# One selective-scan kernel: the outputs of two batch groups and the direct sums gathered in one PSUM bank

## What is computed

```python
dA  = jnp.exp(delta[..., None] * A)                  # 512 channels x 16 states
dBu = delta[..., None] * Bm[:, :, None, :] * xc[..., None]
def step(h, inp):
    da, dbu, c = inp
    h = da * h + dbu
    return (h, jnp.einsum('bdn,bn->bd', h, c))       # y of this step
_, ys = jax.lax.scan(step, h0, (dA, dBu, Cm))        # over 5 steps
y = ys + xc * D_skip
return y * jax.nn.silu(z) @ out_w.T
```

## Time and profile before

| what | us |
|---|---|
| median of 3 runs | 506.29 (503.71 to 507.09) |
| span of the profiled execution | 503.2 |
| scan, loop and its ends | about 291 to 438 of the span |
| after the scan | about 440 to 503.2 |

### The profile page before, as it was taken

How to read it: one execution, slowest core, us unless ns; L and a number is a source line. 1 busy time by engine, 2 the same in 40 slices (tenths; PEclk the granted TensorE clock), 3 DMA queues, 4 the chain that set the end, 5 groups by cost and what they waited for, 6 DMA issues and landing times.

```text
span 503.2 us, 6897 instructions
## 1 busy us (share of the span) xinstructions
PE 452.2 (90%) x1816; PEld 228.5 (45%) x1816; DVE 372.6 (74%) x709; ACT 236.0 (47%) x419; POOL 168.6 (34%) x164
## 2 busy tenths in 40 slices
PE   6999999999999999899967837988898888799997
PEld 3554655655554466477544501222222212275654
DVE  0257576566567668564999976899999999988756
ACT  1143323213221423355886945788887888421100
POOL 6000000100100021405450014889898989422000
PEclk9999999999999999997688977899999999999999
DMA  9992039100000000312026573366546655530000
GB/s 266 313 286 70 1 104 302 42 1 0 0 2 0 0 1 0 119 40 78 2 74 194 146 211 87 109 192 182 157 140 186 195 160 158 141 101 11 10 12 21
DMA packets 36344, 51.75 MB, mean 103 GB/s; under 512 B 5922, under 2 KB 26926, under 8 KB 36320
## 3 DMA queue, kind: packets, MB, share of 16 engines
q1 hardware_dynamic: 34736, 49.86, 33.9%
q10 hardware_dynamic: 1584, 1.59, 1.0%
HBM read 34.59 MB, written 16.52 MB: 102 GB/s over the span
## 4 chain that ended last, share of the span: by engine, by line
PE 33%; DVE 7%; SPq 6%; issue 5%; DMA 4%; ACT 3%; POOL 1%; DVEq 0%; POOLq 0%
PE ps L2072 7%; PE ps L1719 4%; PE ps L2039 4%; PE ps L1015 4%; DMA brows<-bparts 3%; PE ps L1672 3%; PE ps L1028 2%; PE ps L1685 2%; PE ps L1694 2%; SPq L1533 2%; PE ps L1060 2%; DVE da L1894 1%; PE ps L1703 1%; SPq L1007 1%; SPq L1610 1%
## 5 line engine op out<-in xcount | busy, mean ns | idle before, releaser
L1864 POOL TENSOR_TENSOR gb<-da,hb 128x512 f32<-128x512 f32 x62 | 77.8, 1277 | 61.7 <-ACT da L1784 55.2
L1784 ACT ACTIVATE da<-da 128x512 f32<-128x512 f32 x128 | 78.9, 629 | 24.8 <-DVE da L1894 20.4
L1894 DVE TENSOR_TENSOR da<-ps,expA 128x512 f32<-128x512 f32 x128 | 84.0, 686 | 7.8 <-PE ps L1672 7.1
L330 PE MATMUL ps<-area,convw 128*128 128x384 f32 (+1 forms) x220 | 73.4, 486 | 0.6 <-ACT peT L570 0.6
L397 PE MATMUL ps<-wall,peT 128*128 128x512 f32 x144 | 67.8, 593 | 0.0
L1672 PE MATMUL ps<-drows,selb 96*128 96x512 bf16 x128 | 48.5, 401 | 11.6 <-DVE da L1894 5.1
L330 PEld LDWEIGHTS ps<-area,convw 128*128 128x128 f32 (+1 forms) x220 | 41.2, 190 | 28.3 <-issue 1.4
L1685 PE MATMUL ps<-urows,brows 96*128 96x512 bf16 x96 | 35.0, 394 | 13.7 <-DVE gb L1901 7.6
L578 ACT ACTIVATE kvs<-ps 128x512 f32<-128x512 f32 x36 | 21.5, 597 | 52.6 <-PE ps L397 52.6
L570 ACT ACTIVATE peT<-ps 128x384 f32<-128x384 f32 x24 | 11.8, 491 | 66.4 <-PE ps L330 58.7
L1672 PEld LDWEIGHTS ps<-drows,selb 96*128 96x128 bf16 x128 | 11.4, 98 | 61.4 <-DVE da L1894 49.7
(11 more groups left out here) (242 smaller groups left out, 774.8 us busy)
## 6 DMA issues: line engine op xcount, KB each, us to landing
area<-in_xT SPq DMA_DIRECT2D x11, 768.0 KB
yscr<-yst SPq DMA_DIRECT2D x28, 208.0 KB
brows<-bparts SPq DMA_DIRECT2D x16, 240.0 KB, 3.0
drows<-dparts SPq DMA_DIRECT2D x14, 192.0 KB, 2.9
uparts<-pt SPq DMA_DIRECT2D x18, 128.0 KB, 2.4
dparts<-pt SPq DMA_DIRECT2D x18, 128.0 KB, 2.4
urows<-uparts SPq DMA_DIRECT2D x15, 144.0 KB, 2.9
inw<-in_in_wT SPq DMA_DIRECT2D x2, 1024.0 KB
```

The source lines that it names most:

```text
L330: mm = pe.matmul(bank(T_EMB + j % 2, 0, EN), convw[0:n, k, h * P:(h + 1) * P], xbuf[0:n, q, k, c * EN:(c + 1) * EN], start=(k == 0), stop= ...
L1784: act.activation(da_at(q, j), da_at(q, j), ACT.Exp, scale=-1.0).then_inc(da_ready, 1)
L1864: pool.tensor_tensor(gb_at(q, j), da_at(q, j), state, ALU.mult).then_inc({2: m2_done, 3: m3_done, 4: m4_done}[s_], 1)
L1894: dve.tensor_tensor(da_at(q, j), bank(j % 2), expA[:, j % 2, :], ALU.mult).then_inc(e_free, 1)
```

## The change

Outputs of both groups of a pair and the direct sums accumulate in the same bank. `cst` becomes 32 columns wide for each step: group q of a pair writes its C into columns 8q to 8q+8 of it, the rest is zero (set once by POOL before the scan). The four matmuls of q = 0 start the sums, those of q = 1 add to them, and `direct` adds its own into rows 16 to 31 of each block of 32 in bank 6. ACT copies the whole bank once per pair and k, at 128 rows, and `copy_direct` is gone. SP stores per pair: `store_y(i-1, 1)` in the first half, `store_y(i, 0)` and `store_k(i)` in the second; 14 transfers of 256 KB in place of 28 of 208 KB. In the last pair `send_y` carries the pair's 16 rows with one DMA for each j, and SP's order is `store_y(6, 1)`, the four DMAs of `gather_y(0)`, the four of `gather_y(1)`, then `send_y(0)`; after the loop follow the sends of k = 1. `yst` moves into the idle tile `inw`. The diff, cut to its core:

```diff
-        cst = sb("cst", [P, 2, 2, L + 1, GB], ctx=scn)
+        cst = sb("cst", [P, 2, 2, L + 1, 32], ctx=scn)
-            eng.wait_ge(landing(d, s_), 48 if s_ == 3 else 96)
+            eng.wait_ge(landing(d, s_), 32 if s_ == 3 else 64)
-        def send_y(eng, src, g, k, some=(0, 1, 2, 3)):
-            eng.wait_ge(y_copied[k], g + 1)
+        def send_y(eng, k, some=(0, 1, 2, 3)):
+            eng.wait_ge(y_copied[k], NPAIR)
...
-                eng.dma_start(ytok[g * GB:(g + 1) * GB, d, token(s_, d), :],
-                              src[32 * j:32 * j + GB, k, :]).then_inc(landing(d, s_), 16)
+                eng.dma_start(ytok[(NPAIR - 1) * PB:NPAIR * PB, d, token(s_, d), :],
+                              ylast[32 * j:32 * j + PB, k, :]).then_inc(landing(d, s_), 16)
...
-                    if last and q == 0:
-                        send_y(sp, yst, g, 0)
-                        store_y(g - 1, 1)
-                        gather_y(0, (0, 1, 2))
+                    if q == 0 and not first:
+                        store_y(i - 1, 1)
+                    if q == 0 and last:
+                        gather_y(0)
                     elif last:
-                        send_y(sp, ylast, g, 0)
-                        gather_y(0, (3,))
                         gather_y(1)
-                    else:
-                        store_y(g, 0)
-                        if not (first and q == 0):
-                            store_y(g - 1, 1)
-                    if q == 1 and not last:
+                        send_y(sp, 0)
+                    elif q == 1:
+                        store_y(i, 0)
                         store_k(i)
...
             def direct(i):
                 pe.wait_ge(da_ready, 16 * i + 16)
-                need(pe, y_copied[2], i)
...
-                        mm = pe.matmul(ps[o:o + GB, 5 * 512:6 * 512], cst[:, q, d, L, :], da_at(q, 6 + d),
-                                       start=True, stop=True)
+                        sums = cst[:, q, d, :, :].rearrange("p t m -> p (t m)")[:, 32 * L - PB:32 * L + PB]
+                        mm = pe.matmul(ps[o:o + 32, 6 * 512:7 * 512], sums, da_at(q, 6 + d),
+                                       start=False, stop=True, skip_group_check=True)
...
-            def outputs(g, q, k):
-                need(pe, y_copied[k], g)
+            def outputs(g, q, k, i):
+                if q == 0:
+                    need(pe, y_copied[k], i)
...
-                    mm = pe.matmul(ps[32 * j:32 * j + GB, (6 + k) * 512:(7 + k) * 512], cst[:, q, d, token(s_, d), :],
-                                   gb_at(q, 4 * k + j), start=True, stop=True)
+                    mm = pe.matmul(ps[32 * j:32 * j + 32, (6 + k) * 512:(7 + k) * 512], cst[:, q, d, token(s_, d), :],
+                                   gb_at(q, 4 * k + j), start=(q == 0), stop=(q == 1 and k == 1), skip_group_check=True)
...
-            def copy_y(g, k):
-                act.wait_ge(y_done[k], g + 1)
+            def copy_y(i, k):
+                act.wait_ge(y_done[k], 2 * i + 2)
+                if k == 0:
+                    act.wait_ge(y_done[2], i + 1)
...
-                    copy_y(g, 0)
                     if after:
                         exponential(g + 1, 1 - q, 2)
                     if q == 1:
-                        copy_direct(i)
+                        copy_y(i, 0)
                     if after:
                         exponential(g + 1, 1 - q, 3)
-                    if not (first and q == 0):
-                        copy_y(g - 1, 1)
+                    if q == 0 and not first:
+                        copy_y(i - 1, 1)
...
+            pool.wait_ge(xt_ready, NI)
+            pool.memset(cst[:, :, :, :, :], 0.0).then_inc(cleared, 1)
```

More of the change, by code:

```diff
@@ L1490, in tower @@
         y_done = [sem(f"y_done{k}") for k in range(3)]
-        y_copied = [sem(f"y_copied{k}") for k in range(3)]
+        y_copied = [sem(f"y_copied{k}") for k in range(2)]
         y_stored = [sem(f"y_stored{k}") for k in range(3)]
@@ L1516, in tower @@
         Y_ORDER = [(2, 3, 0, 1), (1, 0, 3, 2)]
[L1518 to L1519 removed]
+        PB = 2 * GB
+        def send_y(eng, k, some=(0, 1, 2, 3)):
+            eng.wait_ge(y_copied[k], NPAIR)
             for n in some:
@@ L1522, in send_y, with sums_row @@
                 d, s_ = j % 2, 2 * k + 1 + j // 2
-                eng.dma_start(ytok[g * GB:(g + 1) * GB, d, token(s_, d), :],
-                              src[32 * j:32 * j + GB, k, :]).then_inc(landing(d, s_), 16)
+                eng.dma_start(ytok[(NPAIR - 1) * PB:NPAIR * PB, d, token(s_, d), :],
+                              ylast[32 * j:32 * j + PB, k, :]).then_inc(landing(d, s_), 16)
+        def sums_row(q, d):
+            return 32 * (2 * q + d) + PB + q * GB
         def load_delta(sp, g, q, lo_, hi_, landed=None):
@@ L1592, in scan_sync, with store_y @@
         def scan_sync(sp):
-            def store_y(g, k):
-                sp.wait_ge(y_copied[k], g + 1)
-                sp.dma_start(yscr[bass.ds(g, 1), k], yst[0:NY, k, :]).then_inc(y_stored[k], 16)
+            def store_y(i, k):
+                sp.wait_ge(y_copied[k], i + 1)
+                sp.dma_start(yscr[bass.ds(i, 1), k], yst[:, k, :]).then_inc(y_stored[k], 16)
             def gather_y(k, some=(0, 1, 2, 3)):
-                sp.wait_ge(y_stored[k], 16 * (NG - 2))
+                sp.wait_ge(y_stored[k], 16 * (NPAIR - 1))
                 for n in some:
@@ L1601, in gather_y @@
                     d, s_ = j % 2, 2 * k + 1 + j // 2
-                    sp.dma_start(ytok[0:(NG - 2) * GB, d, token(s_, d), :],
-                                 yscr[0:NG - 2, k, 32 * j:32 * j + GB, :]).then_inc(landing(d, s_), 16)
+                    sp.dma_start(ytok[0:(NPAIR - 1) * PB, d, token(s_, d), :],
+                                 yscr[0:NPAIR - 1, k, 32 * j:32 * j + PB, :]).then_inc(landing(d, s_), 16)
             def store_k(i):
-                sp.wait_ge(y_copied[2], i + 1)
                 for q in range(2):
                     for d in range(2):
-                        o = 32 * (2 * q + d)
-                        sp.dma_start(kscr[d, bass.ds(i, 1), q], kst[o:o + GB, :]).then_inc(y_stored[2], 16)
+                        o = sums_row(q, d)
+                        sp.dma_start(kscr[d, bass.ds(i, 1), q], yst[o:o + GB, 0, :]).then_inc(y_stored[2], 16)
             def gather_k():
@@ L1758, in body @@
                         spread_delta(g + 1, 1 - q, 1)
-                    outputs(g, q, 0)
+                    outputs(g, q, 0, i)
                     if after:
@@ L1769, in body @@
                     if not (first and q == 0):
-                        outputs(g - 1, 1 - q, 1)
+                        outputs(g - 1, 1 - q, 1, i)
                     if after:
@@ L1775, in scan_tensor @@
             pairs(pe, body)
-            outputs(NG - 1, 1, 1)
+            outputs(NG - 1, 1, 1, NPAIR - 1)
             pe.wait_ge(e_free, 2 + 8 * NG)
@@ L1784, in exponential @@
                 act.activation(da_at(q, j), da_at(q, j), ACT.Exp, scale=-1.0).then_inc(da_ready, 1)
-            def copy_y(g, k):
-                act.wait_ge(y_done[k], g + 1)
-                if isinstance(g, int) and g == NG - 1:
-                    act.activation(ylast[0:NY, k, :], bank(6 + k, p=NY), ACT.Copy).then_inc(y_copied[k], 1)
+            def copy_y(i, k):
+                act.wait_ge(y_done[k], 2 * i + 2)
+                if k == 0:
+                    act.wait_ge(y_done[2], i + 1)
+                if isinstance(i, int) and i == NPAIR - 1:
+                    act.activation(ylast[:, k, :], bank(6 + k), ACT.Copy).then_inc(y_copied[k], 1)
                     return
-                act.wait_ge(y_stored[k], 16 * g)
-                act.activation(yst[0:NY, k, :], bank(6 + k, p=NY), ACT.Copy).then_inc(y_copied[k], 1)
+                need(act, y_stored[k], 16 * i)
+                if k == 0:
+                    need(act, y_stored[2], 64 * i)
+                act.activation(yst[:, k, :], bank(6 + k), ACT.Copy).then_inc(y_copied[k], 1)
             def stage_c(g, q, i):
@@ L1796, in stage_c @@
                 need(act, y_done[2], i)
-                act.activation(cst[:, q, :, :, :].rearrange("p d t b -> p (d t) b"),
+                if isinstance(g, int) and g == 0:
+                    act.wait_ge(cleared, 6)
+                act.activation(cst[:, q, :, :, q * GB:(q + 1) * GB].rearrange("p d t b -> p (d t) b"),
                                CT[:, :, :, bass.ds(g * GB, GB)].rearrange("p d t b -> p (d t) b"),
@@ L1804, in copy_state @@
                 act.activation(hb[:, 1, 1, :], bank(4), ACT.Copy).then_inc(h2_copied, 1)
-            def copy_direct(i):
-                act.wait_ge(y_done[2], i + 1)
-                need(act, y_stored[2], 64 * i)
-                act.activation(kst[0:NY, :], bank(5, p=NY), ACT.Copy).then_inc(y_copied[2], 1)
             for j in range(4):
@@ L1830, in body @@
                     if q == 1:
-                        copy_direct(i)
```

(15 more changed lines are left out.)

14 lines of the change are left out of this document (5 added, 9 removed).

## The result

The changed kernel took 515.37 us (median of 5 timed runs), the kernel before 504.20 (median of 5): ratio 1.0213, 95% interval 1.0165 to 1.026. That is slower, in the direction of the sum (+3.95 us), but outside the range of 505.0 to 513.0; the prediction gave "slower by over 1%" a chance of 0.28 and "the same" 0.68.

What follows compares the result with a forecast made beforehand. DVE was taken to set the loop's pace and PE the time after the scan. Loop −1.4, later projection +3.95 and clock loss 1.4 summed to +3.95 us, so 510.3 us as a median, range 505.0 to 513.0.

Steps and rivals of the forecast that it cites:

- seven more of 224 KB at 255 GB/s take 0.90 us each: Hand-over: after the first gather lands at 434.1, seven more end at 440.4, with the two sends behind them.
- where I said 4.55: Hand-over: DVE's first `y_sum` moves from 436.45 to 441.0, 4.55 us later.
- the upper bound of 5.15: Hand-over: latest landing of the sends, 441.6, from a gather's lag under load of 3.7 us.
- 0.6 us to spare: Start of the projection: PE's spare matmuls outlast DVE's gating by 0.6 us, so the projection starts 3.95 us later.
- The clock: PE's pause after its spare matmuls: a short half-speed stretch costs 1.4 us, up to 1.7.
- Rival 4: After the hand-over: a long half-speed stretch costs 6.8 us on top of +2.55, giving 515.6; chance 0.05.
- −1.4 us for eight pairs: Loop: waits for brows and waits on PE go, 1.4 us gained in all (0 to 2.6).
- my 1.0: Loop: rows loaded earlier remove PE's four waits for brows, 1.0 us gained; bounds 0 and 1.4.
- The wider blocks: Loop: 32 weight columns for 8 cost 0, since the eight loads run beside the matmuls.
- Rival 3: Loop: wider tiles cost PE 0.16 us a block, +3.8 in all, giving 512.7 to 514.1; chance 0.10.
- the prediction's own signs of being wrong: Changed profile: L1479 starting without waiting, halves dropping near 8.0 us, or blocks getting longer.
- The 0.4 us for waits taken off PE: Loop: of about 23 waits dropped from PE, eight ahead of the k = 0 blocks count, 0.4 us gained; bounds 0 and 1.2.

Runs made afterwards that it cites:

- b_gather7: Kernel before, its own order, each gather reading 16 rows from each of the first 7 groups, wrong tokens: 505.23 us, ratio 1.0023.
- a_sends_first: Changed kernel with the four sends of k = 0 issued before the gathers of k = 1: 506.04 us, ratio 1.0027.
- a_early_copy: Changed kernel, sends before the gathers of k = 1, the last pair's direct sums in bank 5 and copied by themselves: 508.97 us, ratio 1.0076.
- b_sends_last: Kernel before with only SP's order of the changed kernel in the last pair, eight gathers then the sends: 512.89 us, ratio 1.0175.
- a_gather16: Changed kernel with each of the eight gathers reading 112 rows in one piece, wrong tokens: 509.19 us, ratio 1.0097.
- a_apart_first: Changed kernel with stores as four DMAs of 16 rows, gathers reading one piece, sends before the gathers of k = 1: 506.46 us, ratio 1.0047.
- a_sends_act: Changed kernel with the four sends of k = 0 issued by ACT behind its copy, SP going on with the gathers: 511.03 us, ratio 1.0096.

## Why the prediction was wrong

Taken together, the time from the first gather's issue to DVE's first `y_sum`:

| kernel | gathers ahead of the sends | engines (share) | us |
|---|---|---|---|
| before | 3 | 14 | at most 6.0, no wait |
| b_gather7 | 3 | 7 (0.45) | 8.21 |
| a_sends_first, a_early_copy | 4 | 7 | 10.31, 10.29 |
| b_sends_last | 8 | 14 (0.80) | 11.41 |
| a_gather16 | 8 | 16 (1.01) | 11.35 |
| a_apart_first | 4 | 16 (0.93) | 6.68 |
| a_sends_act | 5 or 6 issued earlier, on the other queue | 7 | 10.90 |
| the changed kernel | 8 | 7 (0.44) | 17.40 |
| predicted | 8 | 14, taken from before | 10.6 |

The two cases on seven engines with four and eight gathers give (17.40 − 10.31) / 4 = 1.77 us for a gather, about twice the 0.90 of the sum.

**The step that failed** is the term "seven more of 224 KB at 255 GB/s take 0.90 us each". The mechanism was right: the sends wait behind the gathers' data. The rate was read from the gathers of before, and the change alters those gathers as well, from 14 groups of 8 rows to 7 pairs of 16. I costed them as the same transfers because their bytes are the same. With 14 engines the step would have held: b_sends_last waits 5.31 us where I said 4.55, just past the upper bound of 5.15 that the landing at 441.6 gave. With 7 engines it was 11.04. Neither bound could hold that, since both took the lag of a transfer on the old number of engines.

One more reading was off, and it works the other way. The prediction gave PE 0.6 us to spare at the start of the projection. PE starts 1.95 us after `y_sum` in the changed kernel (452.07 − 450.12) and started 3.03 us after it before (439.48 − 436.45), so there were 1.08 us to spare: counted from DVE's last product, `y_sum` came 11.12 us later and PE 10.04.

**The clock.** It fell, as forecast, for 2.1 us instead of 1.4. PE's pause was 10 us and not 4; after the 4.16 us pause of b_sends_last the loss was 1.6. The pause alone doesn't decide whether the clock falls: a_early_copy paused for 2.84 us and lost it, a_sends_first for 2.86 and kept it. Rival 4's long loss did not come, although its 515.6 lies next to the result: the profile has a wait in that place, not 6.8 us of slow matmuls.

**The loop.** I said −1.4 us for eight pairs. The five pairs from DVE's start at 342.30 to 424.08 take 81.78 us, before 82.21 (339.34 to 421.55): −0.43. Three parts of it can be checked.
- The waits for brows went: drows of a pair is issued 3.33 us after the start of the first half (362.00 − 358.67), before 4.49 (360.31 − 355.82), so 1.2 us earlier, and no wait is left. Over 8.23 us, the second halves of before held 0.83 us of excess in those five pairs, where all four waits lay (0.9 if the last is held against 8.14, since it is 0.1 us shorter than the others in the changed loop too); my 1.0 was about the right size for that execution.
- The wider blocks took it back: 5 × 0.09 = 0.45 us, 0.7 for eight pairs. I put this at 0 because the loads run beside the matmuls. They do, and a load takes 108 ns where I had drawn 107; it is the matmuls and the blocks that are longer, by some 0.02 us a block. Rival 3 was right in kind; its 3.8 us is five times what the width costs. Longer blocks were one of the prediction's own signs of being wrong, and the halves were to stay at 8.25 us or less: neither held.
- The 0.4 us for waits taken off PE is not to be seen.

The waits for brows also differ between executions of the same loop: b_gather7, whose loop is untouched, ran five pairs in 81.78 us, b_sends_last in 82.25. The changed loop ran them in 81.76 to 81.79 in the seven kernels that leave it as it is. The gain is thus that the loop is steady, 0 to 0.5 us in five pairs. The whole scan, from its first product by A to its last product, took 139.84 us where it took 141.09. That −1.25 looks like the forecast −1.4, but 0.84 of it lies in the first two pairs (44.35 for 45.19), which took 44.47 to 45.19 in the kernels with an untouched loop and 44.18 to 44.79 in the seven others: most of the likeness is chance.

**What held.** ACT's copies are 16 and freed time on ACT that nobody wanted (busy 12.28 us in 353.30 to 369.80, before 13.76). The memset took 0.74 us in an idle stretch of 34.83. The stores changed nothing outside. PE was idle before its first L2029, and DVE's first `y_sum` was released by a DMA to `ytok`, both as said.

**The account.** In the profiles: later start of the scan +3.80, first two pairs −0.84, five pairs −0.43, the last pair up to its last product +0.02, tail +12.15; together +14.7, the difference of the two spans. In the tail, PE starts the projection 14.28 us after the start of DVE's last product, before 4.24 (439.48 − 435.24), so 10.0 later, and loses 2.1 to the clock: 12.1. The medians differ by 11.2.

## What to carry to other kernels

When an edit changes the shape of a buffer, every transfer that reads it is a new transfer: write down the outermost count of both of its sides before and after, for it decides on how many DMA engines the bytes go, and don't carry its old rate over. A small urgent transfer that is spread over all engines is done when its slowest part is done, so it must not be issued behind large ones, above all where these sit on a few engines. Look then at what is on the critical path: 24 fewer copies and 14 fewer stores were worth at most 0.5 us in five pairs, the exchange of two lines of DMA issues nine.

## What the runs showed of the hardware

- The same 224 KB in gathers ran at a DMA share of 0.44 to 0.48 with an outermost count of 7, at 0.78 to 0.84 with 14, and at 0.93 to 1.09 as 112 rows in one piece. The rates were 139 to 177, 255 to 260 and 263 to 294 GB/s: from 7 engines to 14 the rate rose by about half, from 14 to 16 by 15% at most.
- A 32 KB send behind eight gathers on seven engines had 9 of its 16 parts down about 2 us after its issue and the last after 10.14 us. Sent from ACT's queue, the two sends waited for were in 6.57 us after the first one's issue (432.33 to 438.90); from SP's, behind four gathers, 5.99 (432.25 to 438.24).
- Gathers that read one piece are also cheaper to issue: 3.72 us for eight against 6.53.
- A block of four column groups costs 1.06 us with 32 columns of weights and 1.04 with 8, weight loads 108 against 87 ns.
- PE's granted clock fell to half (1.2 GHz) near 447, in a pause of 10 us that began at 442.1, and was full again from about 457, with work under way since 452.07; with 15 spare matmuls in the pause it stayed at full speed, with 12 it fell.
